# Attention scores from Q and K by four row tiles, all probability turns by DMA, values in bursts

## What is computed

```python
q, k, v = x_hat @ Wq.T, ctx @ Wk.T, ctx @ Wv.T    # x_hat: layer norm of x
s = (q_h @ k_h.T) * SCALE                         # per head, 256 x 256, causal
y_h = softmax(s) @ v_h
x1 = x + tanh(g_xattn) * (y @ Wo.T + bo)
out = x1 + tanh(g_ffn) * experts(layernorm(x1))   # router, top 6 of 8, shared expert
```

## Time and profile before

| | us |
|---|---|
| median of 3 executions | 1888.84 (1888.53 to 1889.84) |
| the profiled execution | 1888.26 |
| its span in the trace | 1886.5 |

### The profile page before, as it was taken

The page is one execution under the profiler, slowest core; times in us unless marked ns, Lnnn a source line. Parts: engine busy times, 40 slices in busy tenths (PEclk is TensorE's granted clock), DMA queues, the critical chain, the costliest instruction groups (busy, mean ns, idle before and its releaser), DMA issues.

```text
span 1886.5 us, 32878 instructions
## 1 busy us (share of the span) xinstructions
PE 1836.9 (97%) x11316; PEld 1554.4 (82%) x11316; DVE 1475.1 (78%) x3241; ACT 968.9 (51%) x2260; POOL 798.4 (42%) x1043
## 2 busy tenths in 40 slices
PE   6999999999998999999999999999999999999999
PEld 6899999999997678888778887877888887888887
DVE  6788988888887777777877777797777777877776
ACT  5787888888888533333433343343333434433332
POOL 3445555555445433443534343453343453333330
PEclk9999999999998999999999999999999999999999
DMA  7888898999984422121141211113212112311111
GB/s 227 178 189 195 198 204 190 213 207 192 205 208 99 136 64 69 56 67 56 34 145 54 81 67 56 46 46 133 87 39 88 45 56 77 104 54 57 45 46 45
DMA packets 207429, 205.60 MB, mean 109 GB/s; under 512 B 104224, under 2 KB 159520, under 8 KB 207264
## 3 DMA queue, kind: packets, MB, share of 16 engines
q1 hardware_dynamic: 207264, 203.50, 42.0%
HBM read 111.43 MB, written 18.87 MB: 69 GB/s over the span
## 4 chain that ended last, share of the span: by engine, by line
PE 72%; DVE 11%; issue 5%; SPq 3%; POOL 3%; ACT 2%; DMA 2%; DVEq 0%; POOLq 0%; ACTq 0%
PE gate_up L1310 31%; PE down L1824 18%; PE bank L807 14%; SPq L388 2%; DVE ops_lo L1167 2%; PE scores L910 2%; DVE acc L1675 2%; PE probs_t L944 2%; POOL hidden L1523 1%; DMA turned<-halves 1%; PE rows_t L797 1%; PE y L934 1%; PE y L932 1%; SPq L404 1%; PE down L1803 1%
## 5 line engine op out<-in xcount | busy, mean ns | idle before, releaser
L1310 PE MATMUL gate_up<-xo_hi,ops_hi 128*128 128x512 f32 x1120 | 440.5, 393 | 14.2 <-DVE gated L1286 5.4
L1310 PE MATMUL gate_up<-xo_hi,ops_lo 128*128 128x512 f32 x1120 | 436.6, 390 | 0.0
L1310 PE MATMUL gate_up<-xo_lo,ops_hi 128*128 128x512 f32 x1120 | 436.5, 390 | 0.0
L1310 PEld LDWEIGHTS gate_up<-xo_hi,ops_hi 128*128 128x128 f32 x1120 | 210.5, 188 | 68.0 <-DVE gated L1286 10.6
L1675 DVE SCALAR_TENSOR_TENSOR acc<-down,scale,acc 128x512 f32<-128x512 f32 x320 | 238.2, 745 | 35.0 <-PE down L1824 34.4
L616 ACT ACTIVATE probs<-probs,neg_max 128x128 f32<-128x128 f32 (+1 forms) x512 | 229.2, 449 | 69.4 <-DVE neg_max L739 65.2
L1824 PE MATMUL down<-d_hi,h_hi 128*128 128x512 f32 x640 | 249.1, 389 | 0.0
L1824 PE MATMUL down<-d_hi,h_lo 128*128 128x512 f32 x640 | 249.1, 389 | 0.0
L1824 PE MATMUL down<-d_lo,h_hi 128*128 128x512 f32 x640 | 249.1, 389 | 0.0
L1310 PEld LDWEIGHTS gate_up<-xo_lo,ops_hi 128*128 128x128 f32 x1120 | 210.5, 188 | 44.2
L1310 PEld LDWEIGHTS gate_up<-xo_hi,ops_lo 128*128 128x128 f32 x1120 | 210.6, 188 | 42.4
(11 more groups left out here) (191 smaller groups left out, 4438.9 us busy)
## 6 DMA issues: line engine op xcount, KB each, us to landing
g_raw<-in_w_gate SPq DMA_DIRECT2D x40, 512.0 KB, 3.8
u_raw<-in_w_up SPq DMA_DIRECT2D x40, 512.0 KB, 3.8
d_raw<-in_w_down SPq DMA_DIRECT2D x40, 512.0 KB, 3.7
k_stack<-k_hi SPq DMA_DIRECT2D x128, 128.0 KB, 2.7
q_stack<-q_hi SPq DMA_DIRECT2D x128, 128.0 KB, 2.5
c_in<-in_ctx_t SPq DMA_DIRECT2D x16, 512.0 KB, 4.3
x_in<-in_x SPq DMA_DIRECT2D x16, 512.0 KB, 5.3
k_stack<-k_lo SPq DMA_DIRECT2D x64, 128.0 KB, 2.8
```

Source lines behind the costliest of these rows:

```text
L1310: ins = pe.matmul(gu_ps[bank][:], ops[x][:, which, a, c, :], xo[y][:, b, c, :], start=(begins and c == 0 and i == 0), stop=(c == CH - 1 an ...
```

## The change

Scores: no stacks. For four heads of a group at once, each on its own 32 partitions of the Q and K parts and with its own PSUM bank, three passes of 8 matmuls (2 row tiles, 4 heads) are issued in slots 0, 4, 8 and 12. `q_parts` and `k_parts` are double. DVE takes the maxima of four heads in those slots (MAXIMA); the ring of `probs` holds 6.

Turning: all heads go by ACT, POOL and a DMA transpose; from head 232 on (LATE_HEADS) DVE does POOL's split. Values: four heads in one burst of 36 matmuls, in slots 9, 13, 1 and 5 (PV_LAG 9), into one bank `y_ps` instead of two, so a burst waits for the close of the group before it. A group is closed one slot after its burst (slots 10, 14, 2 and 6). PSUM for transposed probabilities is gone, so y is always turned in `rows_ps`.

Slots: the x load goes from 3 to 6, the residual's from 2 to 4, the context's from slot 14 of the iteration before to 9, bias from 6 to 8, LN_SLOT from 7 to 10, XN_SLOT from 10 to 13. At the change to the expert stage the first two loads of weights keep slot 12, GATE 1 comes ahead of DOWN 0, and DOWN 0 waits for the last values.

```diff
-    TWO_BANKS = H * (B - 2) + 8
-    SPLIT_LAG, TURN_LAG, TR_LAG, PV_LAG = 1, 2, 3, 5
-    GROUP_LAG = PV_LAG + JH
-    RES_LOAD, X_LOAD, C_LOAD, ROWS_LOAD = 2, 3, 14, 14
-    K_STACK, Q_STACK = (5, 6, 7, 8), (9, 10, 11, 12)
+    LATE_HEADS = H * (B - 2) + 8
+    SPLIT_LAG, TURN_LAG, PV_LAG = 1, 2, 9
+    GROUP_LAG = PV_LAG + 1
+    MAXIMA = ((0, 1, 2, 3), (), (), ())
+    RES_LOAD, X_LOAD, C_LOAD, GATE_LOAD, ROWS_LOAD = 4, 6, 9, 12, 13
...
-    LN_SLOT, C_SLOT, XN_SLOT = 7, 12, 10
-    RES_SLOT, MOMENTS_SLOT, STD_SLOT, HAT_SLOT = 6, 0, 2, 6
+    LN_SLOT, C_SLOT, XN_SLOT = 10, 12, 13
+    RES_SLOT, MOMENTS_SLOT, STD_SLOT, HAT_SLOT = 8, 0, 2, 6
...
-                    if s == C_LOAD and has(i, 3):
-                        sp.wait_ge(c_lo_made, far.times(1))
-                        sp.dma_start(c_in[:], row(c_v, far)).then_inc(c_loaded, DMA)
+                    if s == C_LOAD and has(i, 2) and has(i, 0):
+                        sp.wait_ge(c_lo_made, ln.times(1))
+                        sp.dma_start(c_in[:], row(c_v, ln)).then_inc(c_loaded, DMA)
...
-                    if has(i, 0):
-                        dve.wait_ge(scores_done, i.times(H, s + 1))
-                        k = head(i, s)
-                        if k >= RING:
-                            dve.wait_ge(p_lo_made if by_dma(k - RING) else pt_done, nth(k - RING) + 1)
+                    for ahead in MAXIMA[s % JH] if has(i, 0) else ():
+                        h = s + ahead
+                        k = head(i, h)
+                        dve.wait_ge(scores_done, k + 1)
+                        if k >= RING and on_pool(k - RING):
+                            dve.wait_ge(p_lo_made, k - RING + 1)
...
+            def group_scores(i, g):
+
+                q, k = q_parts[i.parity()], k_parts[i.parity()]
+                pe.wait_ge(k_lo_made, i.times(2, g // PAIR + 1))
+                pe.wait_ge(q_lo_made, i.times(2, g // PAIR + 1))
+                wait(pe, max_made, head(i, JH * g))
+                for n, (a, b) in enumerate(PASSES):
+                    for t in range(T):
+                        for j in range(JH):
+                            rows_of = slice(DH * j, DH * (j + 1))
+                            ins = pe.matmul(scores_of(j, t), q[a][rows_of, g, tile(t)], k[b][rows_of, g, 0:P * (t + 1)],
+                                            start=(n == 0 and t == 0), stop=(n == len(PASSES) - 1), skip_group_check=True)
+                            if n == len(PASSES) - 1 and t == T - 1:
+                                ins.then_inc(scores_done, 1)
+
+            def group_values(b, g):
...
+                wait(pe, y_made, b.times(H // JH, g))
+                for hg in range(JH):
+                    h = JH * g + hg
+                    k = head(b, h)
+                    pe.wait_ge(p_turned[k % HALVES], DMA * (k // HALVES + 1))
...
             def run(i):
                 for s in range(H):
...
+                    if has(i, 0) and s % JH == 0:
+                        group_scores(i, s // JH)
+                    if (bh := lagging(i, s, PV_LAG)) and bh[1] % JH == 0:
+                        group_values(bh[0], bh[1] // JH)
                     units(i, s)
```

More of the change, by code:

```diff
@@ L326, in hat_tile, with on_pool @@
         return k if 0 <= k < HATS * T else None
[L328 to L338, removed]
+    def on_pool(k):
+        return k < LATE_HEADS
     def scores_of(k, t):
[L342 removed]
+        return sc_ps[k % JH][:, P:2 * P] if t == 0 else sc_ps[k % JH][:, 2 * P:]
     def probs_of(k, t):
@@ L584, in run @@
                                 act.wait_ge(done, n.times(2, u + 1))
-                                if u == 0 and (not isinstance(n.r, int) or n.k > 0):
-                                    m = n + -1
-                                    for j in range(JH):
-                                        act.wait_ge(stacked[m.parity()][j], m.over(2).times(STACK_DMAS * DMA, STACK_DMAS * DMA))
+                                if u == 0 and n.k == 1:
+                                    act.wait_ge(w_lo_made, N_RAW)
+                                elif u == 0:
+                                    wait(act, scores_done, n.times(H, -H))
                                 act.copy(hi[:, PAIR * u:PAIR * (u + 1), :],
@@ L900, in run @@
             def run(i):
                 for s in range(H):
-                    if has(i, 0):
-                        par = i.parity()
-                        if s < JH:
-                            pe.wait_ge(stacked[par][s], i.over(2).times(STACK_DMAS * DMA, STACK_DMAS * DMA))
-                        wait(pe, max_made, head(i, s) - 1)
-                        pairs = slice(0, 3 * DH)
-                        for t in range(T):
-                            keys = slice(0, P * (t + 1))
-                            ins = pe.matmul(scores_of(head(i, s), t), q_stack[par][pairs, s % JH, s // JH, tile(t)],
-                                            k_stack[par][pairs, s % JH, s // JH, keys], start=True, stop=True)
-                        ins.then_inc(scores_done, 1)
@@ L936, in run @@
-                    if (bh := lagging(i, s, TR_LAG)) and not by_dma(head(*bh)):
-                        j = head(*bh)
-                        pe.wait_ge(probs_made, j + 1)
-                        if j == TWO_BANKS:
-                            pe.wait_ge(yt_lo_made, T * (B - 2))
-                        elif j >= 2:
-                            wait(pe, pt_lo_made, nth(j - 2) + 1)
-                        for k in range(3):
-                            ins = pe.transpose(pt_bank(j)[:, tile(k)], probs[j % RING][:, tile(k)], ident[:])
-                        ins.then_inc(pt_done, 1)
+                    if has(i, 0) and s % JH == 0:
+                        group_scores(i, s // JH)
```

181 lines of the change are left out of this document (70 added, 111 removed).

## The result

| | before | after |
|---|---|---|
| median us | 1889.1 (4 executions, 1888.53 to 1889.84) | 1911.67 (4, 1911.37 to 1914.91) |
| ratio | | 1.0122, 95% interval 1.011 to 1.0134 |
| the profiled execution, its span | 1888.26, 1886.5 | 1914.91, 1912.9 |

The change makes the kernel 22.6 us slower, where 6 us faster was forecast.

The account below looks back on a forecast made before the run. PE set the pace; after the change a chain through ACT, DVE and POOL would stall it, a batch 21.8 + 3.0 + 11.8 = 36.6 us. Thirteen batches +3 and +2, ends -1, -5, -5: 1888.3 - 6 = 1882 us, range 1848 to 1914.

Parts of the forecast that it names:

- the chain: End of slot 9 to slot 14's O half, through ACT, DVE and POOL: 11.8 us, stalling PE 3.6 us.
- score groups: Four groups of 24 32-row matmuls a batch on PE, 1.0 us each, bounds 0.7 and 2.9.
- Rival B: Row tiles overlap little in the scores, so slower: 1901 us at 1.46 a group, 1930 at 2.2; chance 22%.
- rest of the batch: PE's halves, units, values, transposes and three score groups outside the chain: 21.8 + 3 S us.
- S: PE time of one group of scores for four heads, taken as 1.0 us.
- I checked what else could be late in that rest: Outside the chain, DVE's maxima were in time and ACT's 21.4 us fitted PE's 24.8, under 1 us of slack.
- batch 0: First batch: waits for the same Newton chain and then for c_lo, 1 us faster.
- batch 14: No statistics to wait for, so 34 us instead of 39.3: 5 us faster.
- batch 15 and the start of the experts: ACT's sum of 28 us, last transpose some 6 us later, against 37.6 before: 5 us faster.
- A: The chain is not late and PE stays the bound: -43 on 13 batches, -11 at the ends, 1835 us; chance 12%.
- C: Stalls at slots 12 and 14 drop the clock: 1.7 us and more a batch, 1904 us; chance 7%.
- D: Over the whole kernel, the chain and added POOL load cancel all, also at the ends: 1889 us; chance 6%.

Follow-up runs that it names:

- The kernel with slot 11: Changed kernel with heads copied, statistics in slot 7, normalising in slot 11, the experts' signal ahead of the store, late halves alternating between POOL and DVE: 1851.48 us.
- with copies: Changed kernel with each head's turning DMA replaced by a straight copy on the same queue, slot and waits, the base of the experiments: 1906.71 us.

## Why the prediction was wrong

**Right: the chain.** 11.5 us measured for 11.8 forecast, each link within 0.26 us; pauses at slots 12 and 14 of 1.3 and 1.6 us, forecast about 1.7 each; DVE waits 3.05 us for POOL's third part, forecast about 2. The kernels with the statistics in slot 7 and with Newton in slot 11 show it as cause and not only as company: in both the pause at slot 14 goes.

**Right: score groups.** 0.89 us with the drain, 0.63 first to last, forecast 1.0 with bounds 0.7 and 2.9. Rival B falls; had the heads not overlapped, 1.90 us a group. The choice nearer the low end came out; of its two reasons, banks and lanes, no run shows which holds. A change to the 32-row matmuls and back costs little: 0.21 us from the last K or Q matmul to the first score, where the next one would follow after 0.12, and 0.26 from the last score to the next matmul, where scores follow each other after 0.03. That is 0.3 us a group, 1.3 a batch, in which the drain that the Trainium skill (TensorEngine Tiling (Array Packing), Key Properties) speaks of has to lie.

**Wrong: the term "rest of the batch", 21.8 + 3 S.** With S = 0.89 it gives 24.5; measured 37.80 - 11.5 = 26.3, 1.8 us more in each batch, while the chain was 0.3 us shorter than forecast. Against the forecast the 13 batches are 14 us longer (+19 for +5), the last batches 15 us, batch 0 3 us: together the 32.4 us from -6 to +26.4. Either of the first two alone would have turned the sign. Three parts of the 1.8 us:
- The sentence "I checked what else could be late in that rest" looked at the maxima and at ACT, not at the normalising that moves along with the statistics, to slot 13 beside POOL's c_lo. In the trace of the kernel before it takes 0.53 us; it takes 1.96 there (80 to 565 us, 26 of them). The residual and the next x transposes stand behind it: PE waits (5.4 + 2.3)/13 = 0.6 us a batch in the changed kernel. The experiment that shortens c_lo gives 0.8 a batch, and 16 us between the medians. The contention was there before the change, in another place: the scaling of y (L698), 1.13 us in the median and up to 1.91, of which one of 1.11 us stands beside POOL's split of 0.92, takes 0.52 now. I read from the earlier trace rows that y's scaling would be relieved and didn't ask who would be stretched instead. The Trainium skill states the rule (SBUF — State Buffer, section "SBUF: two separate sides"): VectorE and GpSimd share one pair of ports as an exclusive lock held for a whole instruction, taken by a DVE instruction in a two-port mode or, against a GpSimd instruction that reads SBUF, with two SBUF inputs. The traces agree, with the shift of 1.08 us that ends with POOL's 1.15, though none shows the mode of a DVE instruction; and t_lo, which reads PSUM, keeps its 0.68 us beside a POOL instruction of 1.09 (277.22, statistics in slot 7). Read ahead of the prediction, it would have asked for the POOL row beside every DVE row that moves.
- PE's own work was put 1.0 us too low, over the whole batch. The kernel with slot 11 has a batch of 34.0 with 0.4 us of waits, so 33.6, where the sum has 32.6 with S = 0.89. A row of four transposes costs 0.39 on the mean instead of 0.32, a K or Q unit 1.51 for 1.46, a half of V 1.52 for 1.44. Some three quarters of PE's work lie in the rest, so about 0.75 of the 1.8 us come from here (an estimate).
- The clock and the waits for turned heads, which the sum put at nothing in the batches: 3.8 and 1.7 us in the profiled execution, 0.4 us a batch.

**Wrong: batch 0, -1.** It is +2.2. The order is the cause here too: with the statistics in slot 7 it is -3.5 (71.62 against 75.11).

**Right: batch 14**, -5 forecast, -5.1 measured.

**Wrong: batch 15 and the start of the experts, -5.** It is +10.3. The step said 28 us by ACT's sum, and the runs show that the engines' sums are the smaller part here. With copies it takes 63.0 us with DVE full, 62.9 with POOL full and 60.8 with neither, while a shorter transfer of each head gives 4.3 us on top. PE at a clock of 0.63 also takes 1.13 us for 24 score matmuls in three of the four groups, and not 0.63. Before, the heads from 232 on went by PE transposes without a DMA (TWO_BANKS; the DMA share in batch 15 is 0.16); after, each needs a transfer of some 3.5 us, a burst needs four heads, and PE waits 3.9 us for the last one among the experts' first products. "The last transpose lands some 6 us later, with the first two products run before it" had that wait in it at no cost. Each part is read from one execution.

**Rivals.** A: PE bound, 1835; not so here, but its sentence that program order forbids it was the key: with another order, and with copies, the kernel is at 1851. C happened in four of 13 batches of the profiled execution (0.95 or 0.96) at 0.9 us each, not in all at 1.7; in the last batches the clock fell as well. D fits no stretch.

## What to carry to other kernels

When a change moves a step to another slot, list everything that moves with it and lay each beside what the other engines do in that slot: a short instruction that waits for nobody can take nearly four times as long. Where work is taken from the bound engine, look for the fixed order that was hidden by it; moving the statistics and the load that feeds them by three slots was worth 46 us here (1906.7 to 1860.6, both with copies), twice the loss that the change brought. At the ragged end of a pipeline count one item's latency besides the sums of the engines.

## What the hardware showed that I had not expected

- DVE's normalising of 512 columns takes 0.53 us, or 2.80 for the first of the two while POOL subtracts 1024 columns beside it (2.41 us), 1.97 on the mean, and 0.82 on the mean when POOL's works on a quarter of the columns. With POOL's moved away it took 0.54. A shift of two columns took 1.08 us. DVE isn't reported as waiting; its instruction is long. The first normalising starts 0.11 us ahead of POOL's c_lo in all 13 batches of the changed kernel, and is held all the same; with the short c_lo and the same 0.11 us POOL's was the one held in two of 13. So the recorded starts don't tell which engine goes first when they lie this close.
- 24 matmuls of 32 rows on four row tiles in turn take 0.63 us from first start to last, the same 24 head after head 1.65: 2.6 times.
- The clock fell behind some short pauses of PE and not behind others of the same length. With the statistics in slot 7 the 13 pauses ahead of slot 12 are 1.6 to 2.1 us; behind seven of them the granted clock was 0.52 to 0.72 over the next 3 us, that is, a part of them at the lower of its two levels (1.2 instead of 2.4 GHz), and behind six, with the longest of 2.08 us among them, it stayed at 1.00. Around the pause of 1.94 us that ends at 277.96:

```profile
275.00:278.00 3.00, 1.06 (x26) 0.81 (x25) 3.00 (x4) 2.05 (x7) 3.00 (x3) 1.00 0.79 212
278.00:281.00 3.00, 3.00 (x38) 2.44 (x39) 2.81 (x17) 2.01 (x6) 3.00 (x5) 0.72 0.88 183
281.00:284.00 3.00, 3.00 (x20) 2.52 (x18) 0.43 (x1) 2.91 (x10) 3.00 (x2) 0.71 0.65 148
```

From one of these pauses to the next it is 36.1 to 37.0 us where the clock fell behind the first, and 34.6 to 35.2 where it didn't. So a fall costs about 1.5 us, nearly as much again as the pause. The 36 value matmuls behind the pause above took 1.61 us to the last start, and 0.99 where the clock stayed.
